# Projecting queries and output on scaled 16-bit planes instead of 32-bit ones

## The reference, cut to what matters

```python
q = (h @ wq) ; k = ctx @ wk ; v = ctx @ wv     # h = layernorm(x2); 32 query heads, 8 key/value heads, 128 wide
q, k = rope(q), rope(k)
p = softmax(q @ k.T / sqrt(128) + mask)        # 512 x 1024 per head and batch
x3 = x2 + concat_heads(p @ v) @ wo             # wq: 1024 x 4096, wo: 4096 x 1024
```

## Time and profile before

| what | value |
|---|---|
| three timed runs | 2078.07, 2078.19, 2079.86 us |
| median | 2078.19 us |
| profiled execution, span from first to last instruction | 2076.3 us |
| median of the runs less that span | 1.9 us |
| mean granted clock of TensorE | 0.997 of full |
| HBM read, written | 152.76 MB, 44.04 MB |

### The profile page before, as it was taken

The page is one execution under the profiler, slowest core; times in us unless marked ns, Lnnn a source line. Parts: engine busy times, 40 slices in busy tenths (PEclk is TensorE's granted clock), DMA queues, the critical chain, the costliest instruction groups (busy, mean ns, idle before and its releaser), DMA issues.

```text
span 2076.3 us, 25530 instructions
## 1 busy us (share of the span) xinstructions
PE 2023.1 (97%) x9112; PEld 1520.3 (73%) x9116; DVE 1575.3 (76%) x2880; ACT 1002.6 (48%) x1418; POOL 747.1 (36%) x495
## 2 busy tenths in 40 slices
PE   8999999999899999999999999999999999999899
PEld 6877777887667777777777776777777777777587
DVE  5887786667678877878878788888787877878744
ACT  3432341222365655565555555565555555655400
POOL 1552362511133343443434433334344343342400
PEclk9999999999999999999999999999999999999999
DMA  7543553312978688786887899878687786777712
GB/s 267 171 162 122 186 170 102 133 60 101 325 173 172 140 185 168 148 178 137 190 165 146 198 237 235 192 149 184 141 181 165 151 183 142 172 161 142 206 61 72
DMA packets 654942, 341.11 MB, mean 164 GB/s; under 512 B 574720, under 2 KB 591360, under 8 KB 652768
## 3 DMA queue, kind: packets, MB, share of 16 engines
q1 hardware_dynamic: 654816, 339.48, 67.9%
HBM read 152.76 MB, written 44.04 MB: 95 GB/s over the span
## 4 chain that ended last, share of the span: by engine, by line
PE 78%; DVE 6%; DMA 3%; issue 2%; POOL 2%; ACT 1%; SPq 1%; DVEq 0%; ACTq 0%; POOLq 0%
PE ps L43 26%; PE ps L45 25%; PE ps L44 25%; DMA pT<-pp 1%; PE ps L820 1%; POOL u_sb L1960 1%; DVE t_sb L1164 1%; DVE pp L1524 1%; DVE psb L1507 1%; DMA raw<-in_ctx 0%; SPq L625 0%; DMA sinq<-in_sinq 0%; PE ps L1060 0%; PE ps L1044 0%; PE ps L827 0%
## 5 line engine op out<-in xcount | busy, mean ns | idle before, releaser
L1846 ACT ACTIVATE psb<-psb,st 128x1024 f32<-128x1024 f32 x256 | 295.1, 1153 | 220.7 <-DVE st L1510 220.5
L1524 DVE SCALAR_TENSOR_TENSOR pp<-psb,st,pp 128x1024 f16<-128x1024 f32 x256 | 380.9, 1488 | 5.1 <-ACT pp L1853 3.0
L1507 DVE CUSTOM_DVE_ANT_0 psb<-ps,mask 128x1024 f32<-128x1024 f32 x256 | 313.5, 1224 | 84.7 <-PE ps L45 77.9
L1853 ACT ACTIVATE pp<-psb,st 128x1024 f16<-128x1024 f32 x256 | 293.7, 1147 | 144.9 <-DVE st L1519 143.8
L1996 POOL TENSOR_TENSOR wol<-araw,woh 128x512 fp32r<-128x512 f32 x128 | 167.6, 1310 | 431.9 <-ACT woh L1805 431.8
L1996 POOL TENSOR_TENSOR wql<-araw,wqh 128x512 fp32r<-128x512 f32 x128 | 165.3, 1292 | 331.6 <-ACT wqh L1805 331.6
L1164 DVE TENSOR_TENSOR x_lo<-ps,x_lo 128x512 f32<-128x512 f32 x264 | 181.0, 686 | 51.8 <-PE ps L45 51.8
L43 PE MATMUL ps<-woh,osb 128*128 128x512 f32 x512 | 202.6, 396 | 9.3 <-DVE x_lo L1164 4.1
L43 PE MATMUL ps<-ksb,qsb 128*128 128x512 f32 x512 | 200.5, 392 | 7.5 <-DVE st L1507 4.5
L44 PE MATMUL ps<-wol,osb 128*128 128x512 f32 x512 | 200.2, 391 | 0.0
L45 PE MATMUL ps<-woh,osb 128*128 128x512 f32 x512 | 200.2, 391 | 0.0
(11 more groups left out here) (254 smaller groups left out, 4131.2 us busy)
## 6 DMA issues: line engine op xcount, KB each, us to landing
araw<-in_wq SPq DMA_DIRECT2D x128, 256.0 KB, 4.8
araw<-in_wo SPq DMA_DIRECT2D x128, 256.0 KB, 4.5
k_scratch<-khl SPq DMA_DIRECT2D x32, 512.0 KB, 3.6
ksb<-k_scratch SPq DMA_DIRECT2D x16, 1024.0 KB, 6.0
raw<-in_wv SPq DMA_DIRECT2D x16, 512.0 KB, 4.5
raw<-in_ctxT SPq DMA_DIRECT2D x16, 512.0 KB, 4.6
raw<-in_wk SPq DMA_DIRECT2D x16, 512.0 KB, 5.6
raw<-in_ctx SPq DMA_DIRECT2D x16, 512.0 KB, 4.6
```

The costliest lines, as they stand in the source:

```text
L1507: e.tensor_tensor_reduce(out=psb[:, n % 3, :], in0=pair(n % 2 * 2), in1=mask[:, i, :], scale=1.0, scalar=LOWEST, op0=ALU.add, op1=ALU.max, ...
L1524: e.scalar_tensor_tensor(out=pp[:, r, 1024:2048], in0=psb[:, r, :], scalar=st[:, n // 4 % 4, 16 + i:17 + i], in1=pp[:, r, 0:1024], op0=ALU ...
L1846: e.activation(P, P, ACT.Exp, bias=c[:, 4 + i:5 + i], accum_out=c[:, 8 + i:9 + i]).then_inc(a_exp.sem, 1)
L1853: e.activation(pp[:, r, 0:1024], psb[:, r, :], ACT.Copy, scale=st[:, n // 4 % 4, 16 + i:17 + i]).then_inc(a_ph.sem, 1)
```

## The change

The planes of the query and output products become 16-bit (float16), the products' arrangement stays. Float16 has a narrow range, so the slices are scaled by a power of two first. The factor comes from the mean square of the whole matrix: 64 slices of each matrix are read in addition, ahead of the attention, squared and summed by ScalarE (`square`), added over partitions by TensorE (`square_sums`), and made into a factor by VectorE in small steps (`query_sums`, `query_scale`, `output_sums`, `output_scales`, signals `v_ws`). What else moves:

- ScalarE makes the high plane from the raw slice by a factor; GpSimd first multiplies the raw slice by the same factor in place, then subtracts the high plane.
- h is scaled by 1024 in its layer norm, and its planes are stored and loaded as float16, half the bytes.
- The query's factor is undone in cosq and sinq (two VectorE multiplications in `q_end(0)`), the output's in `wo_add`, now a `scalar_tensor_tensor`.
- The slices have eight places (`araw`, and `araw2` where the squares' buffer was), and are loaded one head earlier, in p = 0 already.

```diff
-W_SLOT = [n % 4 if n < 250 else 2 + n % 2 for n in range(len(W_ORDER))]
+W_SLOT = [n % 4 if n < 8 else n % 8 if n < 248 else 2 + (n - 248) % 6 for n in range(len(W_ORDER))]
+SQUARE_STEPS = sorted([*range(6, 28), *range(38, 60), *range(40, 60)])
+H_SCALE = 1024.0
...
-    wqh = alloc(two, "wqh", [128, 3, 512], F32R)
-    wql = alloc(two, "wql", [128, 3, 512], F32R)
+    wqh = alloc(two, "wqh", [128, 3, 512], F16)
+    wql = alloc(two, "wql", [128, 3, 512], F16)
...
# SyncE
+        def load_square(n):
+            if n > 6:
+                e.wait_ge(a_sq.sem, a_sq[n - 7])
+            w = A["wq" if n < 64 else "wo"][n // 2 % 32]
+            e.dma_start(scan[:, n % 7, :], w[:, n % 2 * 512:n % 2 * 512 + 512]).then_inc(d_scan[n].sem, 16)
...
         for p in range(66):
             if p % 4 == 0:
                 load_k(p // 4 + 1)
-            if 0 < p and 2 * p + 6 < 128:
-                load_w(("q", 2 * p + 6))
-            if has_wo(p + 1) and p < 62:
-                load_w(("o", p + 1, 0))
-                load_w(("o", p + 1, 1))
-            if 0 < p and 2 * p + 7 < 128:
-                load_w(("q", 2 * p + 7))
+            if 2 * p + 8 < 128:
+                load_w(("q", 2 * p + 8))
+            if p < 64:
+                load_w(("o", p + 2, 0))
+                load_w(("o", p + 2, 1))
+            if 2 * p + 9 < 128:
+                load_w(("q", 2 * p + 9))
...
# TensorE: ahead of the first feed-forward ("w"), and in p = 0, w = 1 ("v")
+                e.matmul(ps[:, 7, 0:64], twos[:, :], squares[:, 0:64], start=True, stop=True).then_inc(t_rt.sem, 1)
...
# VectorE
+        def floor_roots(m, what, first):
+            e.wait_ge(v_ws.sem, v_ws[what, first - 1])
+            e.tensor_scalar(sc[:, 6:6 + m].bitcast(I32), sc[:, 3:3 + m].bitcast(I32), 0x7F000000, 1, ALU.bitwise_and,
+                            ALU.logical_shift_right).then_inc(v_ws.sem, 1)
+            e.wait_ge(v_ws.sem, v_ws[what, first])
+            e.tensor_scalar(sc[:, 9:9 + m], sc[:, 6:6 + m], 2.0 ** 63, None, ALU.mult).then_inc(v_ws.sem, 1)
+            e.wait_ge(v_ws.sem, v_ws[what, first + 1])
+            e.reciprocal(sc[:, 12:12 + m], sc[:, 9:9 + m]).then_inc(v_ws.sem, 1)
...
+                e.tensor_scalar(cosq[:, :], cosq[:, :], sc[:, 18:19], None, ALU.mult).then_inc(v_ws.sem, 1)
+                e.tensor_scalar(sinq[:, :], sinq[:, :], sc[:, 18:19], None, ALU.mult).then_inc(v_ws.sem, 1)
...
-            tt(xs, bank(6 + i % 2), xs, ALU.add).then_inc(v_xa.sem, 1)
+            e.scalar_tensor_tensor(out=xs, in0=bank(6 + i % 2), scalar=sc[:, 30 + (q - 2) // 32:31 + (q - 2) // 32], in1=xs,
+                                   op0=ALU.mult, op1=ALU.add).then_inc(v_xa.sem, 1)
...
# ScalarE
+        def square(n):
+            e.wait_ge(d_scan[n].sem, d_scan[n]["s", n])
+            e.activation(scan[:, n % 7, :], scan[:, n % 7, :], ACT.Square, accum_out=squares[:, n:n + 1]).then_inc(a_sq.sem, 1)
...
-            e.copy(w_dst(key, 0), araw[:, W_SLOT[n], :]).then_inc(a_whi.sem, 1)
+            e.activation(w_dst(key, 0), w_raw(n), ACT.Copy, scale=sc[:, 16 + wo:17 + wo]).then_inc(a_whi.sem, 1)
...
         root(("h", 7))
         h_hi(6)
+        for n in range(125, 128):
+            square(n)
         split_w(("q", 3))
...
# GpSimd
-            e.tensor_tensor(w_dst(key, 1), araw[:, W_SLOT[n], :], f32(w_dst(key, 0)), ALU.subtract).then_inc(p_wlo.sem, 1)
+            e.tensor_scalar(w_raw(n), w_raw(n), sc[:, 16 + wo:17 + wo], None, ALU.mult).then_inc(p_ws.sem, 1)
+            e.wait_ge(p_ws.sem, p_ws[n])
+            e.tensor_tensor(w_dst(key, 1), w_raw(n), w_dst(key, 0), ALU.subtract).then_inc(p_wlo.sem, 1)
```

More of the change, by code:

```diff
@@ L404, in build_in @@
     v_h2 = signal("v_h2", range(8))
+    v_ws = signal("v_ws", [("w", j) for j in range(7)] + [("v", j) for j in range(2)] + ["cosq", "sinq"]
+                  + [("v", j) for j in range(2, 12)])
     v_rt = signal("v_rt", [(b, j) for b in range(2) for j in range(8)])
@@ L454, in build_in @@
     p_qlo = signal("p_qlo", heads)
+    p_ws = signal("p_ws", range(len(W_ORDER)))
     v_up = signal("v_up", UP_ON_DVE)
@@ L580, in sync_program @@
                 load_raw(f"x{C_LOAD_AT[s]}")
+            for m in range(64):
+                if SQUARE_LOAD_STEP[m] == s:
+                    load_square(m)
         load_raw("c20")
@@ L646, in load_up @@
             e.dma_start(raw3(k), A["up"][k]).then_inc(d_r3[UP_SLOT[k]].sem, 16)
+        for n in range(64, 71):
+            load_square(n)
         e.wait_ge(t_kv.sem, t_kv[63])
@@ L680, in sync_program @@
             e.wait_ge(d_vhl[o].sem, d_vhl[o].last)
-        load("cosq", cosq[:, :])
-        load("sinq", sinq[:, :])
+        e.dma_start(cosq[:, :], A["cosq"]).then_inc(d_tabq.sem, 16)
+        e.dma_start(sinq[:, :], A["sinq"]).then_inc(d_tabq.sem, 16)
         load_k(0)
@@ L829, in turn_tile, with square_sums @@
             m.then_inc(t_htr.sem, 1)
+        def square_sums(what):
+            if what == "w":
+                e.wait_ge(v_scal.sem, v_scal[0])
+                e.wait_ge(a_sq.sem, a_sq[63])
+                e.wait_ge(v_l0.sem, v_l0[1, 6, 0])
+                e.matmul(ps[:, 7, 0:64], twos[:, :], squares[:, 0:64], start=True, stop=True).then_inc(t_rt.sem, 1)
+            else:
+                e.wait_ge(a_sq.sem, a_sq[127])
+                e.wait_ge(v_ws.sem, v_ws["v", 1])
+                e.wait_ge(v_qr.sem, v_qr[0])
+                e.matmul(ps[:, 7, 0:64], twos[:, :], squares[:, 64:128], start=True, stop=True)
+                e.matmul(ps[:, 7, 64:80], twos[:, :], sc[:, 32:48], start=True, stop=True).then_inc(t_rt.sem, 1)
         def ffn_turn(tile):
@@ L1775, in scalar_program @@
                 root(("f", FFN_NORM_AT[s]))
+            for n in range(64):
+                if SQUARE_STEPS[n] in group:
+                    square(n)
         split_hi("c20")
```

193 lines of the change are left out of this document (152 added, 41 removed).

## The result

The changed kernel takes 2073.61 us (median of 20 runs, 2069.75 to 2077.30), the kernel before 2077.68 us (20 runs): ratio 0.9982, 95% interval 0.9975 to 0.9989. It is 4 us faster; 12 had been forecast. The sign was right, the size a third. The profiled execution has a span of 2070.4 us, against 2076.3; these two differ by 5.9 us and the medians by 4.1, because the profiled execution of the changed kernel lies 1.4 us under its median and that of the kernel before 0.4 us above its own.

The account below looks back on a forecast made before the run. The prediction took the attention to run at TensorE's pace (busy 97% of the span). Its terms, -29.1 + 6 + 4 + 4.3 + 1.9 + 1 = -11.9 us, gave a run of 2066 us, range 2053 to 2090 us for 8 in 10.

Parts of the forecast that it names:

- Keys and values: Stage where ScalarE takes 64 squares in 400 us, loads two steps ahead: nothing to 1 us lost, taken at 1.
- Rival 3: Squares disturb the first 534 us, each of h's eight tiles losing 1.5 us: +12 us, 2078 us, chance 0.11.
- The first feed-forward: Small VectorE steps, two ScalarE squares ahead of a table load, and TensorE's sums: 1.9 us lost.
- the multiplied cos and sin: Two VectorE multiplications between the last query product and the first rope, TensorE waiting: 0.9 us lost.
- The attention's start: cosq and sinq multiplied on VectorE, and SyncE's loads ahead of tile 1's turning: 4.3 us lost together.
- the blocked turning: SyncE issues tile 1's turning behind four loads; `p_hi(4)` comes 5.2 us late and TensorE idles over 5 us.
- Shorter products: Query and output products each 10.8 ns shorter, 48 a head, about 60 heads: 31.1 us won, net -29.1 us.
- The return of 2.0 us: Gain given back on TensorE: three more width switches a head, 11 ns each, over 60 heads.
- GpSimd's multiplication: A 0.75 us product ahead of each of 256 subtractions makes `values` late: 6 us, plus 4 us in heads without slack.
- rival 2: GpSimd's product takes 1.3 us, so the slice's low plane comes too late for P: +13 us, 2091 us, chance 0.17.
- the subtraction slows `p_lo`: In the loop, `p_lo` loses three quarters of its overlap with GpSimd's subtraction: 0.67 us for 0.89 us.
- The signs: Expected in the profile after: longer `p_lo`, pT wait from 4.9 to some 15 us, late turning, 5 us idle near 580 us.

Follow-up runs that it names:

- e1: Changed kernel without the 128 loads and 128 squares for the mean square, sums set to constants: 2056.94 us, ratio 0.9891 to the kernel before.
- e4: Changed kernel with the attention's first four weight loads issued behind tile 4's turning, not ahead of tile 1's: ratio 0.9966 to the kernel before.

## Why the prediction was wrong in size

Forecast and measured, in the three stretches of the table:

| | forecast | measured |
|---|---|---|
| to the first score product | 1 + 1.9 + 0.9 = 3.8 | 12.7 |
| from there to the loop | 3.4 | 5.8 |
| loop and end | -29.1 + 6 + 4 = -19.1 | -24.4 |
| sum | -11.9 | -5.9 |

- **Keys and values, the failed step**: "Nothing to 1 us, taken at 1", with "at a third of its time busy" as the reason. It measured 9.2 us at 400. A share of busy time was taken for free time; in a strict order each pair of squares (0.62 us each, 0.19 for the accumulator) moves a cast for which VectorE, then GpSimd and at last TensorE wait, and the lower clock behind that wait, 2 of the 9.2 us, was no term at all. Rival 3 had the right cause but the wrong place, the tiles of h, and too small a chance; that its price, 12 us, is near the 12.7 is luck.
- **The first feed-forward and the multiplied cos and sin**: 1.9 + 0.9 forecast, 3.5 from 400 to 550.3 us. The number is near, the terms aren't shown: e1 has the same small steps, sums and multiplied cos and sin, and loses nothing there (-2.0 and -2.5 us).
- **The attention's start**: the blocked turning happened as forecast. It went out at 588.13 instead of 564.21 us; half of these 24 us is the lateness of the whole stage, the rest (576.5 to 588.1 us) is the hold, 12 us forecast. `p_hi(4)` came 5 us later than the stage did (593.3 instead of 575.7 us), as forecast. But e4 took this hold away and won nothing: it was one of several, and the small steps of VectorE did not "fall into this idle time".
- **Shorter products**: the 10.8 ns hold, 518 ns a head. The return of 2.0 us was mis-sized: it is 115 to 130 ns a head, 7 us. Three starts in the earlier trace rows did not show that the products behind them are slower too.
- **GpSimd's multiplication**: 1.57 us, not 0.75, and 2.8 us instead of 6 + 4. By the prediction's own sum for rival 2 (threshold 1.0 us) the run had to be slower. The second failed step is "the subtraction slows `p_lo`", applied without its condition: the earlier trace rows show it only where the subtraction had begun first. Already with rival 2's product of 1.3 us the subtraction would begin at 1022.23 us, behind `p_lo` at 1022.09. The 2.8 us come by another way, a later `osb`. The Trainium skill (SBUF — State Buffer, Who interferes with whom) says in the same section that the order of issue, and not the shape of the instruction, decides who blocks. The trace agrees for `p_lo` and the subtraction (1.28 us for `p_lo` that began first, 1.78 us for the subtraction behind it). It does not for the product, which reads SBUF too and had begun first 172 times: `p_lo` took 1.32 us there, 0.05 us more than alone. Between the section's full block and the prediction's three quarters the rows fall nearer to the latter: the subtraction ends at 1036.30 us; a full block would have ended it at 1036.44 (`p_lo` ends at 1035.27, and 1.17 us), three quarters of the 0.75 us overlap at 1036.25.
- **VectorE in the loop**, cost nothing: right. Tail: right within 2 us.
- **The signs**: the turning behind a load came, and TensorE idled near 580 us (3.4 us at 584.2, 2.8 us at 591.6) with the lower clock. `p_lo` became shorter instead of longer, and TensorE's wait for pT went from 4.9 to 3.7 us instead of 15. TensorE did wait for the low plane of a query slice, 4.7 us instead of 0.6; the larger of these waits, 3.3 us at 559.2 us, stands where before it waited 3.0 us for the query.

Two errors of 9 and 5 us with opposite signs left the sign right. The second is itself a difference: the product was priced 7 us too high and the return 5 us too low. So the sign was not right for all of its reasons, and partly by luck.

## What to carry to other kernels

Work added to an engine that is a third busy is not free when its program is one fixed order: cost it, and added loads, by the instruction behind and by who waits for that. A wait called issue that comes back with the loop's period can be a late producer: compare the waiting engine's start with the ends of all that feed it. The price of a collision between two engines needs the order in which they start, and which instruction of each it is.
